# GpSimd's two-operand operations on 512 columns in halves; layer 1's features and state turned in fp32 without splits

## What is computed

```python
# layer 0, per graph: x (128 nodes x 64), mask = adj > 0
h   = relu((x @ W1a)[:, :, None, :] + (x[:, :, None] - x[:, None]) @ W1b + b1)   # node pairs x 192
out = einsum('bjkh,bjk->bjh', h, mask) @ W2 + deg[..., None] * b2
x   = layernorm(x + out)
# layer 1: messages through adj and a GRU cell
m   = relu(x @ W1 + b1); m = relu(m @ W2 + b2); msg = relu(adj @ m)
gi, gh = msg @ W_ih.T + b_ih, x @ W_hh.T + b_hh
r, z = sigmoid(i_r + h_r), sigmoid(i_z + h_z); n = tanh(i_n + r * h_n)
x   = layernorm(x + (1 - z) * n + z * x)
```

## Time and profile before

| | |
|---|---|
| runs of the kernel (3) | 804.32 to 805.43 us, median 804.74 |
| profiled execution | 805.59 us, span 804.1 |
| TensorE's granted clock, mean | 0.991 |
| busy: PE, PE's weight loads | 695.8 us (87%), 568.7 us (71%) |
| busy: VectorE | 762.4 us (95%) |
| busy: ScalarE | 640.9 us (80%) |
| busy: GpSimd | 549.3 us (68%) |
| L1217 and L1196 on VectorE | 333.2 and 291.0 us |
| L1175 on VectorE | 96.2 us in 132 operations |
| L1838, L1831, L1812 on GpSimd | 65.3, 59.0, 41.3 us |

### The profile page before, as it was taken

How to read it: one execution, slowest core, us unless ns; L and a number is a source line. 1 busy time by engine, 2 the same in 40 slices (tenths; PEclk the granted TensorE clock), 3 DMA queues, 4 the chain that set the end, 5 groups by cost and what they waited for, 6 DMA issues and landing times.

```text
span 804.1 us, 37406 instructions
## 1 busy us (share of the span) xinstructions
PE 695.8 (87%) x15984; PEld 568.7 (71%) x15984; DVE 762.4 (95%) x851; ACT 640.9 (80%) x1897; POOL 549.3 (68%) x625
## 2 busy tenths in 40 slices
PE   3768789889898989989899898989989898988885
PEld 2547677677787867768787777878677687867662
DVE  5799999999999999999999999999999999998983
ACT  5746676888888888888988888888988888887654
POOL 5534445677868677786867779696777969575772
PEclk9999999999999999999999999999999999999998
DMA  5533243233334323323323232433223243222000
GB/s 150 146 105 75 83 100 88 62 75 101 75 100 97 86 76 75 104 73 108 95 81 84 66 113 63 121 81 94 75 65 111 68 120 76 56 61 75 2 15 27
DMA packets 33316, 66.86 MB, mean 83 GB/s; under 512 B 5504, under 2 KB 6272, under 8 KB 33152
## 3 DMA queue, kind: packets, MB, share of 16 engines
q1 hardware_dynamic: 33152, 64.48, 30.3%
HBM read 22.52 MB, written 4.19 MB: 33 GB/s over the span
## 4 chain that ended last, share of the span: by engine, by line
issue 44%; PE 28%; DVE 21%; ACT 3%; DMA 2%; POOL 1%; SPq 0%; DVEq 0%; POOLq 0%
PE PS L649 20%; DVE AC L1196 11%; DVE AC L1217 7%; PE PS L903 3%; PE PS L968 2%; PE PS L723 2%; PE PS L886 1%; DMA VA<-VN 1%; DVE WM L1165 1%; ACT VN L1565 1%; DMA bs<-in_rows 1%; POOL MT L1780 0%; DVE AC L1212 0%; DVE DM L1175 0%; ACT YO L1484 0%
## 5 line engine op out<-in xcount | busy, mean ns | idle before, releaser
L1217 DVE SCALAR_TENSOR_TENSOR AC<-PS,AC 128x1152 f32<-128x1152 f32 (+4 forms) x288 | 333.2, 1157 | 11.6 <-PE PS L649 10.7
L1196 DVE SCALAR_TENSOR_TENSOR AC<-PS,AC 128x1152 f32<-128x1152 f32 (+4 forms) x256 | 291.0, 1137 | 1.6 <-PE PS L903 1.3
L649 PE MATMUL PS<-DM,VA 128*64 128x192 fp8e5 (+1 forms) x2048 | 126.4, 244 | 41.4 <-DVE AC L1196 29.5
L649 PEld LDWEIGHTS PS<-DM,VA 128*64 128x64 f16 x2048 | 81.3, 110 | 77.8 <-DVE AC L1196 49.6
L649 PE MATMUL PS<-DM,VB 128*64 128x192 fp8e5 (+1 forms) x2048 | 123.9, 240 | 0.7 <-DVE AC L1212 0.2
L903 PE MATMUL PS<-DM,VB 128*64 128x192 fp8e5 (+1 forms) x1024 | 85.9, 245 | 23.7 <-DVE AC L1217 19.2
L1175 DVE TENSOR_SCALAR DM<-CW 128x1536 uint16<-128x1536 uint16 (+1 forms) x132 | 96.2, 750 | 1.0 <-DMA CW<-WM 1.0
L649 PEld LDWEIGHTS PS<-DM,VB 128*64 128x64 f16 x2048 | 89.5, 110 | 2.6 <-DVE AC L1217 1.5
L1812 POOL TENSOR_TENSOR XE<-XQ,XT 128x512 f16<-128x512 f32 x32 | 41.3, 1289 | 70.2 <-ACT XT L1552 70.2
L1838 POOL TENSOR_TENSOR AC<-AC,SD 128x512 f32<-128x512 f32 (+1 forms) x62 | 65.3, 1063 | 29.4 <-DVE DM L1175 29.4
L903 PEld LDWEIGHTS PS<-DM,VB 128*64 128x64 f16 x1024 | 45.6, 108 | 54.1 <-DVE AC L1217 26.9
(11 more groups left out here) (240 smaller groups left out, 2067.5 us busy)
## 6 DMA issues: line engine op xcount, KB each, us to landing
CW<-WM SPq DMA_DIRECT2D x128, 160.0 KB, 2.8
XQ<-in_xq SPq DMA_DIRECT2D x32, 256.0 KB, 2.7
VA<-VN SPq DMA_DIRECT2D x64, 128.0 KB, 2.3
VB<-VN SPq DMA_DIRECT2D x64, 128.0 KB, 2.3
AT<-in_adjt SPq DMA_DIRECT2D x15, 512.0 KB, 4.6
XN<-in_xn SPq DMA_DIRECT2D x16, 256.0 KB, 4.4
out<-YO SPq DMA_DIRECT2D x15, 256.0 KB, 2.1
WG<-in_wg SPq DMA_DIRECT2D x1, 515.5 KB, 7.5
```

What stands on the lines that cost most here:

```text
L649: last = e.matmul(o[k], lhs[:, k], rhs, **flags)
L1196: e.scalar_tensor_tensor(t, tiles(PS[:, b + p:b + 3, :])[:, :, cols], 0.0, t, ALU.max, ALU.add).then_inc(s["sx"], 1)
L1217: e.scalar_tensor_tensor(t, tiles(PS[:, r, :])[:, :, cols], 0.0, t, ALU.max, ALU.add).then_inc(s["sy"], 1)
```

## The change

In `gpsimd_layer1` and `gpsimd_main` every two-operand operation goes through a new function `twice`, which issues it as two operations, on the first and the second half of dimension 1 of the tile (the columns, or, for three-dimensional tiles, the blocks); only the second raises the semaphore. That holds for the 256-column operations of `scale_u` and `add_u` too, which become two of 128. The splits ahead of `xg` and `yt` go, with ScalarE's and GpSimd's operations and their semaphores, and for units 0 to 14 `xg` and `yt` take the fp32 tiles `X1` and `GT` directly; the empty places of the removed steps in the order stay.

```diff
             step("scale1", 1)
-            step("split_x1")
             yield
...
             if u < NG - 1:
-                step("split_h")
                 yield
...
 (xg, PE)
-                main_unit = s is main and not late(u)
-                if main_unit:
-                    pe.wait_ge(s["x1l"], u + 1)
                 for k in range(c.start, c.stop, 2):
                     o = PS[:, b, F * k:F * k + 128]
-                    if main_unit:
-                        both(o, SQ[:, k:k + 2, :].rearrange("p a n -> p (a n)"), idh[:], start=True, stop=False)
-                        last = both(o, X1l[:, k:k + 2, :].rearrange("p a n -> p (a n)"), idh[:], start=False, stop=True)
+                    if s is main and not late(u):
+                        last = both(o, X1[:, k:k + 2, :].rearrange("p a n -> p (a n)"), ident, start=True, stop=True)
...
 (yt, PE)
-                if main_unit:
-                    pe.wait_ge(s["hl"], u + 1)
...
-                    if main_unit:
-                        both(o, SYf[:, n], BDH[:], start=True, stop=False)
-                        last = both(o, GTl[:, n], BDH[:], start=False, stop=True)
-                    else:
-                        last = both(o, GT[:, n], BDC[:], start=True, stop=True)
+                    last = both(o, GT[:, n], BDC[:], start=True, stop=True)
...
 (ScalarE)
-                e.activation(SYf, GT[:], ACT.Copy).then_inc(s["hh"], 1)
...
-                    e.activation(SQ[:], X1[:], ACT.Copy).then_inc(s["x1h"], 1)
...
 (GpSimd)
+        def in_two(e):
+
+            def twice(o, x, y, op):
+                n = o.shape[1] // 2
+                e.tensor_tensor(o[:, 0:n], x[:, 0:n], y[:, 0:n], op)
+                return e.tensor_tensor(o[:, n:], x[:, n:], y[:, n:], op)
+
+            return twice
...
-                e.tensor_tensor(GT[:], GT[:], GR[:], ALU.mult).then_inc(s["gt"], 1)
+                twice(GT[:], GT[:], GR[:], ALU.mult).then_inc(s["gt"], 1)
...
 (the same in gt_in, gd twice, h twice, split_xg, split_ms, split_x, x_split, scale_u, add_u)
...
-                e.tensor_tensor(X1l[:], X1[:], SQ[:], ALU.subtract).then_inc(s["x1l"], 1)
...
-                e.tensor_tensor(GTl[:], GT[:], SYf, ALU.subtract).then_inc(s["hl"], 1)
```

More of the change, by code:

```diff
@@ L1695, in counting @@
             return count
+        def in_two(e):
[4 more added lines that the diff above has]
+            return twice
         def gpsimd_layer1(e, po, s):
+            twice = in_two(e)
             def power1(u):
@@ L1728, in gt_in @@
                 po.wait_ge(s["gt"], 2 * u + 1)
-                e.tensor_tensor(GT[:], GT[:], M1f, ALU.add).then_inc(s["gt"], 1)
+                twice(GT[:], GT[:], M1f, ALU.add).then_inc(s["gt"], 1)
             def gd(u):
@@ L1734, in gd @@
                 po.wait_ge(s["tanh"], u + 1)
-                e.tensor_tensor(GT[:], XGf[u % 2], GN[:], ALU.subtract).then_inc(s["gd"], 1)
+                twice(GT[:], XGf[u % 2], GN[:], ALU.subtract).then_inc(s["gd"], 1)
                 po.wait_ge(s["gd"], 3 * u + 1)
                 po.wait_ge(s["sig"], 2 * u + 2)
-                e.tensor_tensor(GT[:], GT[:], GZ[:], ALU.mult).then_inc(s["gd"], 1)
+                twice(GT[:], GT[:], GZ[:], ALU.mult).then_inc(s["gd"], 1)
             def h(u):
@@ L1743, in h @@
                 po.wait_ge(s["gd"], 3 * u + 2)
-                e.tensor_tensor(GT[:], GT[:], GN[:], ALU.add).then_inc(s["gd"], 1)
+                twice(GT[:], GT[:], GN[:], ALU.add).then_inc(s["gd"], 1)
                 po.wait_ge(s["gd"], 3 * u + 3)
-                e.tensor_tensor(GT[:], GT[:], XGf[u % 2], ALU.add).then_inc(s["h"], 1)
+                twice(GT[:], GT[:], XGf[u % 2], ALU.add).then_inc(s["h"], 1)
             return {"power1": power1, "gt": gt, "gt_in": gt_in, "gd": gd, "h": h, "power2": power2}
         def gpsimd_main(e):
-            po, s = Lane(e), main
+            po, s, twice = Lane(e), main, in_two(e)
             def setup():
@@ L1785, in split_xg @@
                     po.wait_ge(s["gate"], 4 * u)
[L1786 to L1791, removed]
-                    e.tensor_tensor(X1l[:], X1[:], SQ[:], ALU.subtract).then_inc(s["x1l"], 1)
-            def split_h(u):
-                po.wait_ge(s["hh"], u + 1)
-                po.wait_ge(s["yt"], 2 * u)
-                e.tensor_tensor(GTl[:], GT[:], SYf, ALU.subtract).then_inc(s["hl"], 1)
+                    twice(XGl[:], XGf[u % 2], XGh[:], ALU.subtract).then_inc(s["xgl"], 1)
             def split_ms(u):
@@ L1811, in x_split @@
                 po.wait_ge(s["o0"], q - 3)
-                e.tensor_tensor(XE[q % 4][:, :, nat], XQ[:], XT0[:], ALU.subtract).then_inc(s["xql"], 1)
+                twice(XE[q % 4][:, :, nat], XQ[:], XT0[:], ALU.subtract).then_inc(s["xql"], 1)
             def count(g):
@@ L1830, in scale_u @@
                 po.wait_ge(s["ini"], 2 * q + k + 1)
-                e.tensor_tensor(u, u, NNB[:, 4 * k:4 + 2 * k, :], ALU.mult).then_inc(s["im"], 1)
+                twice(u, u, NNB[:, 4 * k:4 + 2 * k, :], ALU.mult).then_inc(s["im"], 1)
             def add_u(q, k):
@@ L1837, in add_u @@
                     po.wait_ge(s["sy"], 9 * q + 9)
-                    e.tensor_tensor(t[:, h, nat], t[:, h, nat], SD[q % 3][:, h, :], ALU.add).then_inc(s["ad"], 1)
+                    twice(t[:, h, nat], t[:, h, nat], SD[q % 3][:, h, :], ALU.add).then_inc(s["ad"], 1)
             def dgen(t, m):
@@ L1846, in soon @@
                 hints.append((e, e.mark_branch_hint_location()))
-            follow(main_order, {"soon": soon, "setup": setup, "parts": parts, "count": count, "x_split": x_split, "split_x": split_x, "mask": mask, "split_xg": split_xg, "split_ms": split_ms, "split_x1": split_x1, "split_h": split_h, "s_ov": s_ov, "clear": clear, "scale_u": scale_u, "add_u": add_u, "dgen": dgen, **gpsimd_layer1(e, po, s)})
+            follow(main_order, {"soon": soon, "setup": setup, "parts": parts, "count": count, "x_split": x_split, "split_x": split_x, "mask": mask, "split_xg": split_xg, "split_ms": split_ms, "s_ov": s_ov, "clear": clear, "scale_u": scale_u, "add_u": add_u, "dgen": dgen, **gpsimd_layer1(e, po, s)})
         def gpsimd_dense(e):
```

16 lines of the change are left out of this document (3 added, 13 removed), and 2 rows, old and new, of the table MAIN.

## The result

The changed kernel takes **807.8 us** (median of 7 runs, 806.6 to 808.6) where the kernel before takes 804.9 on the same chip (804.3 to 805.9): ratio 1.0033, interval [1.0022, 1.0045]. It is 2.9 us slower. I had predicted 805.2 in a range of 798.5 to 810.5: the time lies in the range, but on the slower side of what can be told from no change, which had a chance of 0.35, and I had taken the gains and the costs to cancel.

What follows compares the result with a forecast made beforehand. VectorE, working 544.7 of 550.0 us, was taken as the bound, with PE late in two stretches. Terms -4.1 (halves), +0.6 (PE rounds), +3.2 (copy behind yt), +0.8 (start, tail) gave +0.5 us: median 805.2, range 798.5 to 810.5.

Steps and rivals of the forecast that it cites:

- (a): VectorE's mask of step 2 at 414.46: 0.95 us lost to GpSimd, hidden because PE is late; nothing gained.
- (b): VectorE's mask 2 at 435.49: 0.51 us lost to GpSimd; the stall goes but gains nothing, as VectorE waits for PE.
- (c): VectorE's mask 3 at 438.15: 0.64 us lost to GpSimd, on the path; halves gain 0.08.
- (d): VectorE's word shift at 443.05: 0.44 us lost to GpSimd, on the path; would end at 443.96 instead of 444.30.
- the 0.13 us of the handover: Between GpSimd and VectorE: a waiting VectorE operation gets its turn 0.13 us ahead of GpSimd's recorded end.
- yt in fp32 by way of ScalarE: ScalarE's Y copy behind yt slips 0.3 us, delaying everything to VectorE's SI: +0.25 a period, +3.2 us.
- New stall of 0.05: VectorE's mask 0 at 433.99: GpSimd's lengthened list runs past its start and delays it 0.05 us.
- the rounds on PE: PE around yt and xg: fp32 turns make the third round late by some 0.04 us, +0.6 us in all.
- start and tail: Start 0 to 0.15 us; in the tail two splits +0.27 and a yt half twice, +0.25 each: +0.8 us.
- Waits thin out: Rival, chance 0.27: mask 3 goes first and unhindered, 0.85 us a period gained instead of 0.34; 799 us.
- The turn costs more: Rival, chance 0.19: fp32 yt and xg make the three PE rounds behind them late, +5.6 us; 811 us.
- Halves hold as one: Rival, chance 0.04: VectorE's mask 3 and word shift wait for both GpSimd halves, +16 us; 821 us.

Runs made afterwards that it cites:

- e9: Kernel before with xg in fp32 and halves only for the two operations of the new state: 800.8 us, ratio 0.9944.
- e2: Kernel before with xg and yt both in fp32 and no halves: 808.6 us, ratio 1.0053.
- e3: Kernel before with only yt in fp32, xg kept in two fp16 parts, no halves: ratio 1.0050.
- e10: Kernel before with xg and yt in fp32, no halves, and one of ScalarE's eight squares of a unit left out: ratio 1.0025.
- e6: Changed kernel with the scaling of the seed part issued whole again, all other halves kept: ratio 1.0024.
- e11: Changed kernel with yt back in two fp16 parts and its split whole; all halves and fp32 xg kept: ratio 1.0005.
- e4: Kernel before with only xg in fp32, yt kept in two fp16 parts, no halves: ratio 1.0000.
- e1: Kernel before with all the halves and nothing else, both fp16 turns and their splits kept: 818.3 us, ratio 1.0168.
- e7: Kernel before with xg in fp32 and halves only for the addition to the sum: ratio 1.0051.
- e5: Kernel before with xg and yt in fp32, no halves, and ScalarE copying VE ahead of YO: ratio 1.0033.
- e8: Kernel before with xg in fp32, halves for the addition to the sum and the new state, VE copied ahead of YO: ratio 1.0008.

## Why the prediction was right and where it was not

**Right.** (a) and (b) were hidden: mask 2 gave back 0.51 and the idle time behind it took 0.52. (c) gave back 0.11 where I had 0.08, (d) 0.23 where I had 0.26. Lock order, the 0.13 us of the handover and the cost of a split held in every case read here. The strict reading of the Trainium skill's page SBUF — State Buffer, section Who interferes with whom (whoever is issued first blocks), carried over to two halves as if they were one block, is not what two GpSimd operations back to back do: VectorE, asking during the first, goes ahead of the second, in the changed kernel (1.08 at mask 3) and in e9 (0.85 at the shift). yt in fp32 by way of ScalarE: +0.25 predicted, +0.26 measured in e2 and e3, and e10 gives 0.21 of it back by shortening ScalarE's list alone. The idle time ahead of SI came as described.

**The step that failed.** "New stall of 0.05 ... that stall is gone, for nothing": I counted mask 0's new stall as hidden, like everything ahead of VectorE's idle time behind mask 2. It measured 0.10, and e6, which removes it, is 0.10 a period faster. The PE stretch behind it starts only when VectorE has done its rounds there, so what delays mask 0 delays the stretch (VectorE's idle time behind mask 2 is 0.84 with the stall and 0.84 without it, in e6, so PE moved along): the round behind it starts 0.10 later against SI, which eats up the 0.11 gained at mask 3, and what is left is the word shift's. Another 0.04 went ahead of SI, where VectorE, coming earlier, waits longer for ScalarE (0.21 against 0.17 in e2). So the halves give 0.20 a period (46.84 - 46.63), not 0.34.

By terms, in us of the whole run, from the distances in the traces: the halves in the steady part -2.5 for -4.1 (12 x 0.205); the rounds on PE 0 for +0.6; yt +3.1 for +3.2 (12 x 0.26); start and tail +1.5 for +0.8. Sum +2.1, where the profiled executions differ by 2.1 and the medians by 2.9; I had +0.5. The +0.6 that was not there made up for part of the 1.6 that the halves failed to give, which is luck.

The start adds 0.4 here, and what of it is the halves' can't be read. From the first to the fifth SI the kernels without any halves lie between 168.2 (e10) and 169.4 (before), the changed kernel at 169.7 and e11 at 169.3. GpSimd's mask of the adjacency, which the first rounds wait for, starts between 27.50 and 28.55 in the kernels without halves and at 29.06 in the changed one, in all of them right behind its DMA; that DMA is issued at 23.11 in the changed kernel, at 22.86 before, and at 23.42 in e2, which has no halves and still starts the mask at 28.25. So it is not the time of issue but mostly the landing that differs, and that part is open. The tail is open too: behind the last SI the changed kernel takes 0.6 longer than e2, but e11 takes 1.5 longer than e4 and e1 1.7 longer than the kernel before, and with yt in fp32 it is 0.5 (e2) and 1.0 (e3) longer than in the kernel before, each from one profile. The halves seem to cost more there than the 0.27 that I had; how much more is not shown.

**What I had not seen.** The two parts are not a sum. I had added up GpSimd's load (+2.5 and -2.3 a period) and called it unchanged, which it nearly is (9.6 us more in 550), but did not ask how much room its list has where something waits for it. Without the removed splits the same halves cost 0.93 a period (e1). And the bound of -13 us for both stalls together was never to be had: (c) can give 0.15 (e7), (d) 0.44, so about 7 us, of which e9 takes 4.7 (12 x 0.39).

**Rivals.** "Waits thin out": its condition, that mask 3 goes first, never came about, not even in e6, where VectorE was 0.10 earlier, since GpSimd's list follows VectorE. "The turn costs more": the kernel is slower, but not by this; the turn costs its +0.26 a period and no more, PE's rounds nothing, and what is missing is missing from the halves. "Halves hold as one": no.

## What to carry to other kernels

A half shortens a wait where the other engine asks for the lock in its first part: so at mask 3 in e7 (0.64 down to 0.10) and at the word shift in e9 (0.44 down to 0.04). That alone does not make it pay. e7 lost, since PE was late behind mask 3 and the splits moved GpSimd into the next meeting; e9 won, since nothing behind the shift took the gain back: VectorE keeps its 0.39 up to the next SI. Two of the nineteen splits of a period give 0.39 a period (e9, against e4), all nineteen give 0.20 (against e2) and cost GpSimd 2.5. Ask of each stall what waits behind it (mask 2, right in front of an idle VectorE, gave nothing; the stall at mask 0, two operations earlier, cost its full 0.10), and of each lengthened list where the next engine waits for it; load over a window does not show that, the distance from the end of an operation to the start of its reader does (GTl to yt, 0.10). Where an unbroken list on another engine slips, moving one copy ahead in it gave back 0.09 of 0.26 and had a price of its own (e5, e8); making the list shorter gave back 0.21 (e10).

## What the runs showed of the hardware that I had not expected

An fp32 turn of 128 columns on PE is hidden at xg although PE's time for it doubles, 0.45 to 0.87 us (e4, ratio 1.0000), and not at yt, where it grows only from 0.22 to 0.44 a half. The halves of one GpSimd operation are two turns at the lock: VectorE's operation, even one of 0.81 us, goes in between, and the pair then ends later than the one piece would have (GT<-GT,XG in e9 from 439.15 to 441.15, 2.00, where in one piece it takes 1.27). GpSimd does not lose by that what it did not lose before, for behind a whole operation the wait falls on the next one: SHL takes 1.25 before and 0.67 in e9. What is behind the halves moves by the splits alone, in e7 by 0.31 for two; and a shift as small as that decides which operation VectorE meets next.
